# Three pace constants in the issue planner of a two-layer AdaLN transformer kernel

## The chip, the cores and the metric

The kernel runs on one core of one Trainium2 chip. The metric is the device time of one execution in microseconds (us), lower is better. Most executions of one kernel agree within 0.3%.

## The reference

The input is a batch of eight elements (called images here), each 1024 tokens of 256 features, in float32. Two transformer layers follow one another; before each part the input is normalised and modulated, and after it multiplied by a gate. Cut to what matters:

```python
# layer 0, attention: windowed ("light") plus routed ("heavy")
h = layernorm(x) * (1 + ca) + sa
light = window_attention(layernorm(h), 8 heads of 64, window 64) @ out_w
idx_q, idx_kv = top_k(coordinate_descent(h @ tok), 256)      # two routings
heavy = attention(rmsnorm(h[idx_q]), rmsnorm(h[idx_kv]), rope, 8 heads + a null key) @ out_w
x = x + ga * (light + null_token.at[idx_q].set(heavy))
# layer 0, feed-forward: 64 small functions of one variable with 16 relus each
x = x + gb * kan(layernorm(x) * (1 + cb) + sb)
# layer 1, attention: 16 heads of 16, causal, per-head layernorm on q and k, rope
x = x + ga1 * (causal_attention(layernorm(x) * (1 + ca1) + sa1) @ Wo + bo)
# layer 1, feed-forward: 256 -> 1024 -> 256, gelu, weights of two values
x = x + gb1 * (gelu(h @ bw1 + b1) @ bw2 + b2)
```

## The kernel before

After a setup of some 235 us (modulation, the routing of all images, the weights), one block of code serves all images. For each image *b* the work is cut into stages, and each stage into steps:

- `light` (windowed attention), `chain` (the end of layer 0 and the head of layer 1 for a quarter of the tokens, four quarters), `att` (causal attention, in two halves), `mlp1` (the last feed-forward, in two halves) belong to image *b*.
- `hrows` (16 steps), `heavy` (58 steps) and `hnorm` (10 steps) prepare the next image while `att` of this one runs. `hrows` gathers the routed rows; `heavy` is the routed attention; `hnorm` normalises the next image's `h`.

A planner in plain Python, `schedule()`, writes all steps of all stages into one list, `ORDER`. Each of the five engines (TensorE as PE, VectorE as DVE, ScalarE as ACT, GpSimd as POOL, and SP, which issues transfers) then issues its own part of each step in exactly this order; `take` walks the list once for each engine. So the list fixes in what order an engine meets its instructions, and semaphores alone decide when they run. An instruction that waits holds up everything behind it on its own engine.

The planner has three lanes and works in rounds. In a round lane 0 (`begin`, `start`, `light`, `att`) receives the credit `PACE`, and lanes 1 and 2 receive `SIDE`; for each full unit a lane appends one step, if its gates allow it, and loses the unit in any case:

```python
if lanes[0]:
    pace = pace_of(lanes[0][0], done.get(lanes[0][0], 0), pace)
    credit += pace
while credit >= 1.0 and lanes[0]:
    turn(0)
    credit -= 1.0
for lane in range(1, 3):
    if lanes[lane]:
        key = lanes[lane][0]
        due[lane] += SIDE[key[0], key[2]] if key[1] or key[0] != "chain" else 1.0
    while due[lane] >= 1.0 and lanes[lane]:
        turn(lane)
        due[lane] -= 1.0
```

In one image's period lane 1 holds `chain 0`, `chain 2`, `mlp1 0`, `heavy` of the next image and `mlp1 1`; lane 2 holds `chain 1`, `chain 3`, then `hrows` and `hnorm` of the next image. For the first image alone `hrows` and `heavy` stand in lane 1 beside `light 0`, and its `hnorm` is part of the setup. A period has 240 rounds. Gates that matter here: `hrows` starts when `mlp1 0` has done 6 steps; `att 1` when `mlp1 0` has done 13; `heavy` when its lane is free and `hrows` has done 12; `hnorm` when `att 1` has done 45 steps and then 11 more turns of its lane (`LAG`) have passed; `mlp1 0` when `chain 3` is done and `att 0` lacks two steps.

What the touched stages issue:

- `hrows`. POOL: steps 0 to 3 gather the four tiles of routed rows `rg` from DRAM (L2501, indirect DMA), steps 4 to 7 the rope rows (L2505), step 8 two small products (L2511, L2512), step 10 a power (L2516). DVE: steps 5 to 8 each wait for one gathered tile and sum its squares (L1820), step 9 a maximum (L1824), steps 12 to 15 scale the tiles (L1829, L1832). SP: a load of two gates at step 0 and a fill of `heavy_d` at step 12 (L2730).
- `hnorm`, twice five steps, once for each half of the tokens. DVE: two steps of statistics (L756), then the aggregate and the variance (L763, L766), then two steps of normalising (L771), which wait for POOL. POOL: at the third step of each five a power (L783), which waits for L766.
- `att 0` has 41 steps. Steps 0 to 16 are the first group's maxima, 17 to 32 the main loop; the last eight are the last product with v, the last normalisation, two transposes and four tiles of the output projection (PE L1695, DVE L2151, POOL L2653). `att 1` has 77 steps: one maximum tile ("fill": PE L1573 with L1578, reduced on DVE by L2070, L2072, L2074 or L2078) in each of the first 36, then 32 steps of the main loop (scores L1615 on PE, exp L2399 on ACT, the causal triangle L2643 on POOL, product with v L1633 on PE). The fills use two PSUM banks in turn, so a fill waits for the maximum of the fill two before it. The main loop takes four groups of eight steps, and the last four steps of a group have two triangles each; at the end of a group ACT copies the result (L2408).
- `mlp1 0` has 24 steps: 8 of normalisation, 8 of the first matrix product (PE L1710, L1711; gelu L2442 on ACT), 8 of the second (PE L1724, 16 matmuls for each of four tiles; DVE L2167; POOL L2667). At its ninth step POOL adds a bias to half the tokens (L2569, L2571).
- `heavy` begins with two memsets on DVE (L1840, L1841) that wait until `mlp1 0` is all added (L2667), and its transposes of the gathered tiles (PE L1365) wait for L1832. Later its pairs of heads are copied by DVE (L1892).

Of the kernel before, what the change touches and what calls it, by code (L numbers as in the profile page):

```python
# [64 lines left out]
def zone(base, start):  # L65
# [3 lines left out]
    def view(shape, dt=F32):  # L69
# [13 lines left out]
}  # L83


PACE = {("light", 0): (1.88, 0.9, 0.9), ("light", 1): (1.0, 1.463, 1.1), ("att", 0): (1.461, 0.9, 0.9, 0.67), ("att", 1): (1.0, 1.15, 1.15, 0.632)}

SIDE = {("chain", 0): 1.0, ("chain", 1): 1.0, ("chain", 2): 1.0, ("chain", 3): 1.0, ("heavy", 0): 1.0,
        ("mlp1", 0): 1.0, ("mlp1", 1): 0.98, ("hrows", 0): 0.8, ("hnorm", 0): 0.8}

FIRST = {('light', 0): (3.01, 0.54), ('light', 1): (1.2, 1.1)}

# [11 lines left out]
def pace_of(key, n, pace):  # L104
    if key[0] == "light":
        f = (17, 12)[key[2]]
        if key[1] == 0:
            return FIRST[key[0], key[2]][n >= f]
        return PACE[key[0], key[2]][(n >= f) + (n >= f + UNITS)]
    if key[0] == "att":  # L110
        f, g = len(first_fills(key[2])) + 1, NG * TH * (key[2] + 1)
        return PACE[key[0], key[2]][(n >= f) + (n >= f + g // 2) + (n >= f + g)]
    return pace
# [160 lines left out]
def first_fills(c):  # L274

    return [(0, *f) for f in fills(c)] + [(1, *f) for f in fills(c)[:AHEAD[c]]]
# [2624 lines left out]
```

## Time and profile before

| what | value |
|---|---|
| median of 3 runs | 4073.16 us (4068.53 to 4076.90) |
| the profiled execution's own time | 4068.53 us |
| its span, first to last instruction | 4066.8 us |
| mean granted TensorE clock | 0.91 |
| busy: PE, DVE, ACT, POOL | 83%, 60%, 48%, 36% |

The profile is of one of the three runs, the fastest. A "span" is the time from its first to its last instruction. Busy shares are averages over stages in which different engines set the pace; the questions here are answered by the order of instructions in short stretches, so most rows are from the timeline: start in us, duration in us, engine, line, operation, tiles and shapes, and in brackets the idle time of the engine before it and what ended that.

### The profile page before, as it was taken

To read this page: it belongs to the slowest core of one execution; us is meant where nothing else is said; L and a number is where in the kernel's file an instruction comes from. 1 tells how busy PE (TensorE), PEld (TensorE's weight loads), DVE (VectorE), ACT (ScalarE), POOL (GpSimd) and SP (SyncE) were. 2 spreads that over 40 slices of the span, in tenths; PEclk is the share of its full clock that TensorE was granted. 3 is DMA by queue.
4 is the path that set the end of the run, shared out by engine and by line. 5 is a ranking of instruction groups with operands and counts; after the bars stand their busy time and mean duration, and the time that the engine had idled before them with its cause. 6 is when DMAs were issued, how large, how long until landed. Compare 5 with 4: busy or idle time off the path is not lost. (4 is left out here: it accounts for less than half of the span.)

```text
span 4066.8 us, 81863 instructions
## 1 busy us (share of the span) xinstructions
PE 3382.8 (83%) x30905; PEld 2021.9 (50%) x30905; DVE 2459.2 (60%) x6188; ACT 1955.7 (48%) x4555; POOL 1476.9 (36%) x1799
## 2 busy tenths in 40 slices
PE   7368778897799878998798977998788987998787
PEld 3235554564446544465545644465444654465444
DVE  6754767466563666547573675637674575736662
ACT  5224444544364544554455542654445543645434
POOL 4123452244423542235422543235422344235411
PEclk8579889998899989998899988999899988999888
DMA  6210230002300123002400023002220024000220
GB/s 235 84 37 14 56 106 28 14 12 64 110 16 25 32 64 84 23 12 56 117 17 14 28 51 108 17 24 55 77 56 16 12 64 111 16 25 21 59 69 7
DMA packets 233603, 207.39 MB, mean 51 GB/s; under 512 B 13776, under 2 KB 214224, under 8 KB 233176
## 3 DMA queue, kind: packets, MB, share of 16 engines
q1 hardware_dynamic: 229168, 192.61, 16.9%
q0 software_dynamic: 3328, 8.39, 0.8%
q8 instruction: 252, 4.13, 0.4%
q14 instruction: 135, 1.11, 0.1%
q10 hardware_dynamic: 720, 1.15, 0.1%
HBM read 123.83 MB, written 77.69 MB: 50 GB/s over the span
## 5 line engine op out<-in xcount | busy, mean ns | idle before, releaser
L2399 ACT ACTIVATE arena<-pb 128x512 f32<-128x512 f32 (+3 forms) x1536 | 663.9, 493 | 239.2 <-PE pb L1615 232.7
L2479 POOL TENSOR_TENSOR arena<-arena,small 128x512 f32<-128x512 f32 x256 | 287.8, 1126 | 475.6 <-DVE small L1791 474.1
L2223 ACT ACTIVATE arena<-arena,small 128x256 f32<-128x256 f32 x512 | 255.8, 500 | 381.0 <-DVE small L1774 380.6
L1573 PE MATMUL pb<-arena 96*32 96x128 bf16 (+5 forms) x5280 | 371.0, 278 | 67.0 <-DVE arena L2078 24.9
L1615 PE MATMUL pb<-arena 98*32 98x512 bf16 (+3 forms) x4608 | 399.7, 340 | 31.0 <-ACT arena L2399 23.1
L1633 PE MATMUL pb<-arena,v 128*17 128x512 f32 (+3 forms) x3072 | 379.3, 498 | 22.0 <-POOL arena L2643 13.7
L2643 POOL TENSOR_SCALAR_AFFINE_SELECT arena<-arena 128x256 f32<-128x256 f32 x512 | 217.3, 428 | 474.3 <-ACT arena L2399 470.5
L2078 DVE TENSOR_REDUCE arena<-pb 128x1 f32<-128x512 f32 x512 | 334.2, 684 | 85.7 <-PE pb L1573 83.4
L1774 DVE CUSTOM_DVE_ANT_0 arena<-pb,wmask 128x256 f32<-128x256 f32 x512 | 195.7, 419 | 214.5 <-PE pb L1310 201.8
L1573 PEld LDWEIGHTS pb<-arena 96*32 96x32 bf16 (+1 forms) x5280 | 183.8, 101 | 250.7 <-issue 62.9
L1310 PE MATMUL pb<-arena 128*128 128x256 f32 x1024 | 282.9, 401 | 5.0 <-issue 2.8
L1287 PE MATMUL pb<-hTf,wqkv 128*128 128x512 f32 (+1 forms) x640 | 245.9, 536 | 23.8 <-DVE hTf L1743 12.1
L1724 PE MATMUL pb<-w2T,arena 128*128 128x256 f32 x1024 | 238.6, 384 | 12.1 <-ACT arena L2442 12.1
L1615 PEld LDWEIGHTS pb<-arena 98*32 98x32 bf16 x4608 | 139.4, 97 | 208.5 <-ACT arena L2399 113.2
L2070 DVE TENSOR_REDUCE arena<-pb 128x4 f32<-128x512 f32 x256 | 171.5, 687 | 110.7 <-PE pb L1573 101.2
L2349 ACT ACTIVATE arena<-arena,cols 128x256 f32<-128x256 f32 x256 | 148.2, 596 | 148.7 <-DVE arena L1988 147.0
L1310 PEld LDWEIGHTS pb<-arena 128*128 128x128 f32 x1024 | 188.4, 196 | 59.3 <-issue 25.8
L1724 PEld LDWEIGHTS pb<-w2T,arena 128*128 128x128 f32 x1024 | 191.3, 191 | 45.4 <-ACT arena L2442 15.8
L2539 POOL TENSOR_TENSOR arena<-arena,small 128x256 f32<-128x256 f32 x128 | 78.4, 612 | 350.8 <-DVE small L1886 349.8
L1320 PE MATMUL pb<-ident,arena 128*128 128x128 f32 x1024 | 162.9, 283 | 49.4 <-DVE arena L1784 29.4
L2072 DVE TENSOR_REDUCE arena<-pb 128x2 f32<-128x512 f32 x256 | 169.4, 685 | 28.2 <-PE pb L1573 27.9
L1578 PE MATMUL pb<-cmask,identb 128*32 128x512 bf16 (+1 forms) x640 | 118.7, 412 | 78.0 <-DMA arena<-split_k 57.1
(339 smaller groups left out, 7123.6 us busy)
## 6 DMA issues: line engine op xcount, KB each, us to landing
arena<-split_q SPq DMA_DIRECT2D x64, 384.0 KB, 3.8
arena<-split_k SPq DMA_DIRECT2D x24, 768.0 KB, 6.7
split_q<-arena SPq DMA_DIRECT2D x64, 192.0 KB, 2.1
split_q<-arena SPq DMA_DIRECT2D x96, 128.0 KB, 1.9
split_k<-arena SPq DMA_DIRECT2D x64, 192.0 KB, 2.2
split_k<-arena SPq DMA_DIRECT2D x96, 128.0 KB, 1.9
arena<-split_k SPq DMA_DIRECT2D x24, 384.0 KB, 8.5
xn<-h_d SPq DMA_DIRECT2D x8, 1024.0 KB, 9.2
```

The source lines that it names most:

```text
L1287: mm = t.matmul(bank[bk][:, 0:hi - lo], wqkv[:, k, col0:col0 + P], hT[:, k, lo:hi], start=k == 0, stop=k == KD - 1)
L1310: mm = t.matmul(bank[bk][:, j * 2 * P:(j + 1) * 2 * P], qt[:, p_, j, i * P:(i + 1) * P], kt[:, p_, i * P:i * P + 2 * P], start=True, stop= ...
L1573: mm = t.matmul(out[r:r + wide], qh[:, q0 + r:q0 + r + wide], kh_, **kw)
L1615: mm = t.matmul(bank[bk][r:r + 32, 0:w_], ka[slot(c, g)][0:KA, h, kt_ * P + r:kt_ * P + r + 32], qa[slot(c, g)][0:KA, h, q0:NH], start=Tru ...
L1633: t.matmul(bank[3][32 * h:32 * h + HD1 + 1, q0:NH], v1[:, kt_, G1 * g + h, :], pp[pn % 4][:, h % 2, 0:w_], start=kt_ == 0, stop=kt_ >= TH ...
L1724: mm = t.matmul(bank[bk][:, 0:D], g1[:, k, i * P:(i + 1) * P], w2T[:, k], start=k == 0, stop=k == FT - 1)
L1774: ins = v.tensor_tensor_reduce(out=sm[n % 2][:, j], in0=bank[n % 2][:, j * 2 * P:(j + 1) * 2 * P], in1=mk, scale=-1.0, scalar=3e38, op0=AL ...
L2078: ins = v.tensor_reduce(m[:, h, i, 3:4], bk, AX_X, ALU.max)
L2223: ins = s.activation(pm[n % 3][:, j], sm[n % 2][:, j], ACT.Exp, bias=nmx[:, 2 * sl + j:2 * sl + j + 1], scale=-1.0, accum_out=sml[:, 2 * s ...
L2399: s.activation(pp[pn % 4][:, h % 2, 0:w_], bank[n % 3][:, 0:w_], ACT.Exp).then_inc(a_exp1, 1)
L2479: g.tensor_tensor(pm[n % 3], pm[n % 3], rcl[:, 2 * sl:2 * sl + 2].unsqueeze(2).broadcast_to([P, 2, 2 * P]), ALU.mult).then_inc(p_norm0, 1)
L2643: g.affine_select(out=p2, in_=p2, pattern=[[0, 2], [1, P]], compare_op=ALU.is_ge, fill=0.0, base=0, channel_multiplier=-1).then_inc(p_tri, 1)
```

## The change

Three numbers of the planner change. Lane 0's pace in the last eight steps of `att 0` goes from 0.67 to 0.72 of a step in each round; the paces of `hrows` and of `hnorm` go from 0.8 to 1.0. No instruction is added, removed or altered; only their order in `ORDER` is.

```diff
-PACE = {("light", 0): (1.88, 0.9, 0.9), ("light", 1): (1.0, 1.463, 1.1), ("att", 0): (1.461, 0.9, 0.9, 0.67), ("att", 1): (1.0, 1.15, 1.15, 0.632)}
+PACE = {("light", 0): (1.88, 0.9, 0.9), ("light", 1): (1.0, 1.463, 1.1), ("att", 0): (1.461, 0.9, 0.9, 0.72), ("att", 1): (1.0, 1.15, 1.15, 0.632)}
 
 SIDE = {("chain", 0): 1.0, ("chain", 1): 1.0, ("chain", 2): 1.0, ("chain", 3): 1.0, ("heavy", 0): 1.0,
-        ("mlp1", 0): 1.0, ("mlp1", 1): 0.98, ("hrows", 0): 0.8, ("hnorm", 0): 0.8}
+        ("mlp1", 0): 1.0, ("mlp1", 1): 0.98, ("hrows", 0): 1.0, ("hnorm", 0): 1.0}
```

## Rows read from the trace of the kernel before

**Rows 1.** The page, part 1: busy us, share of the span, instructions.

```profile
PE 3382.8 (83%) x30905; PEld 2021.9 (50%) x30905; DVE 2459.2 (60%) x6188; ACT 1955.7 (48%) x4555; POOL 1476.9 (36%) x1799
```

**Rows 2.** The waits: waiter, releaser, us in total, times, longest us.

```profile
DVE arena L1820 <- DMA arena<-h_d,idx_all: 48.8, 18, 5.6
```

**Rows 3.** Timeline of POOL, gathers for image 2.

```profile
1065.33 0.99 POOL L2501 DMA_INDIRECT arena<-h_d,idx_all  x1 [0.27 <-POOL xt L2571]
```

**Rows 4.** Timeline of DVE in the same stretch, image 2.

```profile
1069.29 0.69 DVE L2070 TENSOR_REDUCE arena<-pb 128x4 f32<-128x512 f32 x1 [0.69 <-PE pb L1573]
...
1073.22 0.42 DVE L1820 CUSTOM_DVE_ANT_0 arena<-arena 128x256 f32<-128x256 f32 x1 [1.45 <-DMA arena<-h_d,idx_all]
...
1073.57 0.69 DVE L2070 TENSOR_REDUCE arena<-pb 128x4 f32<-128x512 f32 x1
...
1074.24 0.68 DVE L2078 TENSOR_REDUCE arena<-pb 128x1 f32<-128x512 f32 x1
```

**Rows 5.** Timeline of PE, image 2: the second product of `mlp1 0` begins.

```profile
1072.20 3.62 PE L1724 MATMUL pb<-w2T,arena 128*128 128x256 f32 x16
```

**Rows 6.** Timeline of DVE, image 3: the third and the fourth gathered tile.

```profile
1543.27 0.73 DVE L1820 CUSTOM_DVE_ANT_0 arena<-arena 128x256 f32<-128x256 f32 x1 [1.78 <-DMA arena<-h_d,idx_all]
...
1543.94 0.68 DVE L2070 TENSOR_REDUCE arena<-pb 128x4 f32<-128x512 f32 x1
1544.84 0.42 DVE L1820 CUSTOM_DVE_ANT_0 arena<-arena 128x256 f32<-128x256 f32 x1 [0.22 <-DMA arena<-h_d,idx_all]
```

**Rows 7.** Timeline of PE, image 3, the same stretch.

```profile
1544.67 0.39 PE L1573 MATMUL pb<-arena 96*128 96x512 bf16 x1 [1.54 <-DVE arena L2070]
1544.90 3.62 PE L1724 MATMUL pb<-w2T,arena 128*128 128x256 f32 x16
```

**Rows 8.** Timeline of DVE, image 2: `heavy` begins.

```profile
1089.07 0.91 DVE L1840 MEMSET arena<- 64x1024 f32 x1 [0.53 <-issue]
...
1091.24 0.35 DVE L1832 TENSOR_SCALAR arena<-arena,small 128x256 f32<-128x256 f32 x1
...
1098.91 0.74 DVE L1862 SCALAR_TENSOR_TENSOR arena<-pb,sc_all,arena 128x512 f32<-128x512 f32 x1
```

**Rows 9.** Timeline of DVE, image 3: `heavy` begins.

```profile
1561.81 0.91 DVE L1840 MEMSET arena<- 64x1024 f32 x1 [0.30 <-issue]
...
1570.64 0.74 DVE L1862 SCALAR_TENSOR_TENSOR arena<-pb,sc_all,arena 128x512 f32<-128x512 f32 x1
```

**Rows 10.** Windows, images 2 and 3: stretch, length, busy us of each engine, granted clock, DMA.

```profile
1088.00:1099.00 11.00, 7.13 (x35) 2.11 (x37) 6.07 (x11) 1.68 (x4) 0.72 (x1) 0.69 0.35 119
1560.80:1571.80 11.00, 7.27 (x44) 2.00 (x42) 6.79 (x12) 1.68 (x4) 0.68 (x1) 0.84 0.35 119
```

**Rows 11.** Timeline of DVE, image 2: `hnorm` beside `heavy`.

```profile
1197.61 0.69 DVE L1892 COPY arena<-pb 128x512 f32<-128x512 f32 x1 [0.32 <-PE pb L1425]
...
1205.45 0.36 DVE L763 BATCH_NORM_AGGREGATE small<-small 128x2 f32<-128x6 f32 x4
```

**Rows 12.** Timeline of POOL, image 2, the same stretch.

```profile
1199.17 0.41 POOL L2643 TENSOR_SCALAR_AFFINE_SELECT arena<-arena 128x256 f32<-128x256 f32 x1 [0.46 <-ACT arena L2399]
...
1206.33 1.04 POOL L783 TENSOR_TENSOR small<-small,mhalf 128x4 f32<-128x4 f32 x1
```

**Rows 13.** Timeline of PE, image 2, the same stretch.

```profile
1199.78 0.41 PE L1633 MATMUL pb<-arena,v 128*17 128x128 f32 x8
...
1202.64 1.05 PE L1633 MATMUL pb<-arena,v 128*17 128x512 f32 x8 [0.57 <-ACT arena L2408]
```

**Rows 14.** One line, PE L1260: first transposes of images 2 and 3.

```profile
L1260 PE MATMUL pb<-ident,xn x16: 272/272/273, 1228.5 to 1238.2; 128*128 128x128 f32 x16
L1260 PE MATMUL pb<-ident,xn x16: 272/272/273, 1699.9 to 1709.6; 128*128 128x128 f32 x16
```

**Rows 15.** One line, PE L1724: second product of `mlp1 0`, two images on.

```profile
L1724 PE MATMUL pb<-w2T,arena x64: 377/379/381, 1544.9 to 1559.8; 128*128 128x256 f32 x64
L1724 PE MATMUL pb<-w2T,arena x64: 377/379/381, 2010.6 to 2025.5; 128*128 128x256 f32 x64
```

## The prediction

> **What bounds the kernel now.** I began with the page: PE is busy for 83% of the span, more than any other engine [rows 1], so what delays PE tends to delay the end. Then I read the totals of the waits for the stages that the change touches; the one that matters is DVE's wait for gathered rows, 48.8 us in 18 times [rows 2]. Then the timelines of DVE, PE and POOL around `hrows`, `heavy` and `hnorm` for images 1 to 7, of which images 2 and 3 stand for the two patterns there are; then the windows for the clock; last, one line at a time for the distance between stages. The change adds and removes no work, so everything hangs on which instruction stands behind which wait.
>
> **What the new list looks like.** Count rounds from the one in which `mlp1 0` starts, as round 0. At 0.8 `hrows` starts in round 5 and skips every fifth round: in images 2, 4 and 6 its 16 steps fall in rounds 5, 6, 7, 9, 10, 11, 12, 14, 15, 16, 17, 19, 20, 21, 22, 24, in images 3, 5 and 7 in 5, 7, 8, 9, 10, 12, 13, 14, 15, 17 and so on to 24, in image 1 in 6 to 24. At 1.0 they fall in 5 to 20 without a hole. `att 1` takes one step a round from round 13, `heavy` still starts in round 24, since lane 1 is held by `mlp1 0` until then. `hnorm` opens 11 turns after round 56: at 0.8 its ten steps reach from round 69 or 70 to 81 or 82, at 1.0 from 67 to 76.
>
> **Part 1, the fourth sum of squares.** POOL's order around the gathers hardly changes: the bias of `mlp1 0` (round 8, lane 1) still precedes the fourth gather (round 8, lane 2). That gather is issued at 1065.33 [rows 3], and DVE, waiting, starts on it at 1073.22 [rows 4]: 7.9 us. In the old order of images 2, 4 and 6 the sum stands in round 15, behind three of `att 1`'s maxima. In the new one it stands in round 13, behind one. So the maximum that now runs at 1069.29 [rows 4] must wait for the tile. PE feels it: the fourth fill needs the second maximum, the fifth needs the third, and behind the fifth stands the second product of `mlp1 0`. From the sum's start to the next maximum is 0.35 us, to the one after 0.67 more [rows 4]; from that one's start to the product 0.96 (1543.94 to 1544.90) [rows 6, 7]. The product would start at 1073.22 + 1.98 = 1075.20 in place of 1072.20 [rows 5]: 3.0 us late.
>
> Images 1, 3, 5 and 7 pay part of this already. Their third gather stands behind the bias, its tile comes at 1543.27, and PE idles 1.54 us before the fifth fill [rows 6, 7]. In the new order the third tile comes sooner and the fourth takes its place: 1544.84 + 1.98 = 1546.82 against 1544.90 [rows 6, 7], 1.9 us. The fourth tile should also land somewhat sooner than now, as in image 2 (7.9 us from issue), so I take 1.5 us, with bounds 0.8 and 1.9.
>
> Is it given back? Behind the product everything up to `heavy` hangs on it: the memset starts 16.9 us after it in both images (1072.20 to 1089.07, 1544.90 to 1561.81) [rows 5, 7 to 9]. Then the patterns differ. Image 2 needs 9.84 us from the memset to the first value rows, image 3, which came 1.7 us later into its product, 8.83 [rows 8, 9], under a granted clock of 0.69 against 0.84 [rows 10]; of the two levels of 1.2 and 2.4 GHz image 2 spends more of it at the lower. I take 1.0 us back for the three images of that pattern, so 2.0 each; the bounds are 0 and 1.0. Sum of part 1: 3 x 2.0 + 4 x 1.5 = 12 us, bounds 3 x 2.0 + 4 x 0.8 = 9 and 3 x 3.0 + 4 x 1.9 = 17; if the tile is there in time it is nothing, which is a rival below.
>
> At this place the Trainium skill can be weighed. The row shows 7.9 us from issue to use [rows 3, 4]. The skill ("DMA: Bandwidth & Descriptors", Anatomy of one DMA — SWDGE (gpsimd) path) puts a transfer issued by GpSimd at about 2.0 us plus bytes over 436e3; for the 128 rows of 1 KB here that makes an estimate of 2.3 us, the tile would be there before the sum asks for it, and part 1 would cost nothing. The trace does not agree.
>
> **Part 2, the scaling of the tiles.** The last L1832 leaves the place behind `heavy`'s memsets, where it held up the next maximum by 0.35 us less its overlap [rows 8]; I take 0.26 us off in each of seven images: -1.8 us, bounds 0 and -2.4. The other steps of `hrows` move inside the second product, where PE works without a stop and DVE has room; they cost nothing while that is so. SP's fill comes three rounds earlier with nothing queued in between, POOL's power stands before instead of behind the first L2667, which it would hold up only if it came within its 1 us; its input is there at about 1074.4, the L2667 is due after 1078.
>
> **Part 3, the power of `hnorm`.** Its first power (L783) moves from round 72 or 73 to round 69. There it falls between the triangles of the last two steps of the third of `att 1`'s four groups. It waits for DVE's variance, which waits behind the copy of a pair of heads (1197.61) [rows 11]. From the aggregate's start to the power's end is 1205.45 to 1207.37, 1.9 us [rows 11, 12]. The copy ends at 1198.3, so POOL is free at 1200.2, and the last two triangles, the second of which now starts at 1199.17 [rows 12], would start at 1200.2 and about 1200.6. The product that needs them now starts at 1199.78 [rows 13] and would at about 1200.7 for its first pair and 1201.1 for its second. Behind it on PE stand the next scores, and on ACT the copy for which PE already waits 0.57 us before 1202.64 [rows 13]. I take 0.9 us for each of seven images, bounds 0.2 (ACT and PE catch up) and 1.4 (all of it stays): +6.3 us. The places are the same in all seven images. The later steps of `hnorm` move into time in which DVE idles; `start` comes in round 93, so finishing sooner gains nothing.
>
> **Part 4, 0.72 and the first image.** `att 0`'s tail takes about 11.1 rounds in place of 11.9. `mlp1 0` still waits for `chain 3`, so no stage starts sooner; a tile of the output projection slips ahead of one or two steps of `chain 3`. Zero, with 0.5 us to either side for an image. But it also shifts the fraction that lane 0 carries on, which up to now was nearly alike in all images, and so the places of `light` against `chain` in the next one. That has a price: from its first transposes to the second product of the next `mlp1 0` image 2 takes 316.4 us (1228.5 to 1544.9), image 3 310.7 (1699.9 to 2010.6) [rows 14, 15]; images 1, 2 and 7, with a lower fraction, lie at 315 to 316, the other four at 311 to 314. By hand the fractions of the new list spread over all values, about half of them in the better range, as now: 0 us, bounds -9 and +12. In the first image `heavy` starts three rounds sooner beside `light`; 0, bounds -2 and +2.
>
> **The sum.** 12 - 1.8 + 6.3 + 0 = 16.5 us, on 4068.5 for the profiled execution, 4085.0. The median of the three runs lies 4.6 us above that execution; by it, 4089.7. I say 4089.
>
> **The rivals.** (a) Gathers in time: with less in front of them the tiles land before DVE asks, or the PE queue absorbs the wait, and part 1 is worth 2 us or less. For it: the wait depends on what the 16 DMA engines have to do then, and one tile of image 1 was there without a wait. Against: six of seven images show DVE waiting for the fourth tile even in its present, later place, if only by 0.05 to 0.2 us in four of them. Sum 2 - 1.8 + 6.3 = 6.5, so 4080. (b) The power waits harmlessly (0.2 us in each image) and part 1 stands at its lower bound: 9 - 1.8 + 1.4 = 8.6, so 4082. (c) Faster: the fractions put images 1, 2 and 7 into the better range, 3 x 3.1 = -9.4 us, and the gathers land in time. This decides once parts 1 and 3 together stay under 3 us; with part 2, 4062. For it: 5.7 us between images 2 and 3 with the same instructions. Against: my count of the fractions. (d) The same mechanism to the other side: four more images in the worse range, +12.5 on the forecast, 4102. (e) The new list does what it says, but all of it in slack: 4073.
>
> **How the numbers follow.** No change is what lies within 0.2%, 8 us, about what a measurement of this kernel can tell. The forecast 0.47 (its own range 4083 to 4097), (a) and (b) 0.20, (c) 0.14, (d) 0.10, (e) 0.09. Half of (a) and (b) would read as no change, and some of the forecast's low end: slower 0.60, same 0.26, faster 0.14. The range from 4066 to 4105 leaves out about two in ten.
>
> **What would show it.** The step is right if in every image the fourth L1820 stands between the first two L2070 with a DMA wait of some 4 us before it, PE idles 2 to 3 us at the fourth and fifth fill, and L1820's total wait for the DMA grows well past 48.8 us. Part 3 is right if L783 stands before the last two L2643 of the group and L1633 waits for POOL there. The distances of rows 14 and 15, taken for all images, show part 4. Wrong would make it: a tile that lands within 5 us, or a clock that gives the stall back.

## The result and the profile after

The changed kernel is slower: 4098.26 us, median of 6 runs (4087.93 to 4111.07), against 4071.59 us (4068.43 to 4076.90, 6 runs). The ratio is 1.0078, 95% interval 1.0057 to 1.0098, which is 31.8 us on 4071, more than the 26.7 us between these medians. The record holds twelve more executions of the changed kernel, and the median of all 18 is 4102.5 us (4087.93 to 4119.38). The profiled execution took 4090.72 us, 22.2 us more than that of before; it is the second fastest of the 18, so its trace shows less of the loss than a typical execution has. I had forecast 16.5 us for it and 4089 us by the median. The six runs scatter over 23 us, all 18 over 31, those of before over 8. One execution each of `hnorm` alone (5721 us), of the late sums (9700 us) and of the kernel before beside it (9673 us) is left out of the ratios below.

Unless another view is named, rows below are from timelines: start, duration, engine, line, operation, and in brackets the idle time before. First the page after, part 1 (answers to [rows 1]), and under it a row of the totals of waits (answers to [rows 2]).

```profile
PE 3394.9 (83%) x30905; PEld 2029.7 (50%) x30905; DVE 2463.2 (60%) x6188; ACT 1955.4 (48%) x4555; POOL 1478.4 (36%) x1799
```

```profile
DVE arena L1820 <- DMA arena<-h_d,idx_all: 76.5, 27, 5.9
```

The instruction counts are the same, and PE is busy 12 us longer: part of the loss is work that ran slower, not idling. The wait for the gathered rows grew from 48.8 to 76.5 us. Where it went is seen in image 2, on POOL, DVE and PE (answers to [rows 3 to 5]):

```profile
1061.55 0.99 POOL L2501 DMA_INDIRECT arena<-h_d,idx_all  x1 [0.27 <-POOL xt L2571]
```

```profile
1065.54 0.69 DVE L2070 TENSOR_REDUCE arena<-pb 128x4 f32<-128x512 f32 x1
1069.38 0.42 DVE L1820 CUSTOM_DVE_ANT_0 arena<-arena 128x256 f32<-128x256 f32 x1 [3.15 <-DMA arena<-h_d,idx_all]
...
1069.73 0.69 DVE L2070 TENSOR_REDUCE arena<-pb 128x4 f32<-128x512 f32 x1
...
1070.40 0.69 DVE L2070 TENSOR_REDUCE arena<-pb 128x4 f32<-128x512 f32 x1
```

```profile
1070.48 0.56 PE L1578 MATMUL pb<-cmask,identb 128*128 128x512 bf16 x1 [2.55 <-DVE arena L2070]
1070.83 1.06 PE L1573 MATMUL pb<-arena 96*128 96x128 bf16 x5
1071.68 4.76 PE L1724 MATMUL pb<-w2T,arena 128*128 128x256 f32 x16
```

The fourth sum stands between the first two maxima and waits 3.15 us; the fill of PE behind it waits 2.55 us. The last of the three rows was not forecast: the 16 matmuls of the second product take 4.76 us in place of 3.62. The windows show why; columns are the stretch, its length, busy us of PE, PEld, DVE, ACT and POOL, the granted clock, DMA. First after (the stall, then the product's beginning), then before (the product's beginning):

```profile
1067.50:1070.50 3.00, 0.45 (x3) 0.03 (x2) 1.12 (x5) 0.78 (x1) 1.59 (x3) 1.00 1.08 262
1071.60:1075.10 3.50, 3.50 (x12) 2.84 (x11) 1.19 (x2) 0.00 (x0) 0.03 (x1) 0.66 0.62 219
```

```profile
1072.20:1075.70 3.50, 3.50 (x18) 2.99 (x17) 1.70 (x5) 0.78 (x1) 0.55 (x1) 1.00 1.05 270
```

PE was busy 0.45 of 3.00 us in the stall, and in the first 3.5 us of the product the granted clock is 0.66, so that much of them ran at the lower level of 1.2 GHz: 12 matmuls in place of 18.

I then measured the same distances in both traces, for all seven images, and added them up (us):

| stretch | before | after | difference |
|---|---|---|---|
| start to the first product (L1710) of image 1's stretch | 587.3 | 581.7 | -5.6 |
| first product (L1710) to second (L1724), 7 times | 95.7 | 110.1 | +14.4 |
| second product to `heavy`'s memset (L1840), 7 times | 118.3 | 123.9 | +5.6 |
| memset to the next first transposes (L1260), 7 times | 973.2 | 977.2 | +4.0 |
| first transposes to L1710, 6 times | 1801.7 | 1812.0 | +10.3 |
| last first transposes to the end | 490.5 | 484.1 | -6.5 |

The second and third lines hold the stall, the fourth `hnorm`, the last two what `light`, `chain` and `att 0` take. Of the 14.4 us of the second line 10.1 are idle time of PE (9.8 us before, 19.9 after); the rest is matmuls that ran slower.

### The profile page after: what moved, and what is told of

It is laid out like the page before. It is cut to its first block and busy times, and to the rows that moved or that the text cites. A ratio compares the mean times of both kernels' runs of the same rounds, so it can differ in the third digit from the quotient of the medians.

```text
span 4089.0 us, 81864 instructions
## 1 busy us (share of the span) xinstructions
PE 3394.9 (83%) x30905; PEld 2029.7 (50%) x30905; DVE 2463.2 (60%) x6188; ACT 1955.4 (48%) x4555; POOL 1478.4 (36%) x1799
## 3 DMA queue, kind: packets, MB, share of 16 engines
q1 hardware_dynamic: 229168, 192.61, 16.7%
## 5 line engine op out<-in xcount | busy, mean ns | idle before, releaser
L1633 PE MATMUL pb<-arena,v 128*17 128x512 f32 (+3 forms) x3072 | 382.0, 499 | 24.1 <-POOL arena L2643 15.0
L2643 POOL TENSOR_SCALAR_AFFINE_SELECT arena<-arena 128x256 f32<-128x256 f32 x512 | 216.3, 426 | 461.1 <-ACT arena L2399 457.7
L1573 PEld LDWEIGHTS pb<-arena 96*32 96x32 bf16 (+1 forms) x5280 | 185.5, 102 | 246.9 <-issue 71.3
L1287 PE MATMUL pb<-hTf,wqkv 128*128 128x512 f32 (+1 forms) x640 | 246.7, 537 | 24.4 <-DVE hTf L1743 11.5
L1724 PE MATMUL pb<-w2T,arena 128*128 128x256 f32 x1024 | 244.5, 391 | 10.8 <-ACT arena L2442 10.8
L1724 PEld LDWEIGHTS pb<-w2T,arena 128*128 128x128 f32 x1024 | 196.6, 196 | 46.2 <-ACT arena L2442 14.5
L2072 DVE TENSOR_REDUCE arena<-pb 128x2 f32<-128x512 f32 x256 | 169.6, 686 | 26.8 <-PE pb L1573 26.4
```

Source lines behind the costliest of these rows:

```text
L1287: mm = t.matmul(bank[bk][:, 0:hi - lo], wqkv[:, k, col0:col0 + P], hT[:, k, lo:hi], start=k == 0, stop=k == KD - 1)
L1573: mm = t.matmul(out[r:r + wide], qh[:, q0 + r:q0 + r + wide], kh_, **kw)
L1633: t.matmul(bank[3][32 * h:32 * h + HD1 + 1, q0:NH], v1[:, kt_, G1 * g + h, :], pp[pn % 4][:, h % 2, 0:w_], start=kt_ == 0, stop=kt_ >= TH ...
L1724: mm = t.matmul(bank[bk][:, 0:D], g1[:, k, i * P:(i + 1) * P], w2T[:, k], start=k == 0, stop=k == FT - 1)
L2643: g.affine_select(out=p2, in_=p2, pattern=[[0, 2], [1, P]], compare_op=ALU.is_ge, fill=0.0, base=0, channel_multiplier=-1).then_inc(p_tri, 1)
```

## The experiments

Theory P is the prediction's. Theory F, formed on the table above, gives the larger part to the fraction of a step that lane 0 carries into `light` (part 4). The runs below the first were timed beside 24 executions of the kernel before on the same chip; the difference is the ratio, less one, times 4071, and can differ by some us from that of the medians.

| run | median us | ratio, 95% interval | difference us |
|---|---|---|---|
| whole change | 4098.3 | 1.0078 (1.0057 to 1.0098) | +31.8 |
| `hrows` alone | 4098.5 | 1.0060 (1.0046 to 1.0074) | +24.4 |
| `hnorm` alone | 4071.2 | 0.9999 (0.9988 to 1.0009) | -0.4 |
| `att 0` tail alone | 4080.7 | 1.0026 (1.0016 to 1.0037) | +10.6 |
| `hrows` and `hnorm` | 4102.8 | 1.0068 (1.0044 to 1.0092) | +27.7 |
| `hrows`, sums two steps later | 4070.7 | 0.9994 (0.9983 to 1.0006) | -2.4 |
| `hrows`, sums one step later | 4086.9 | 1.0050 (1.0036 to 1.0065) | +20.4 |
| change, bias behind the gather | 4086.8 | 1.0041 (1.0026 to 1.0055) | +16.7 |
| before, fraction 0.42 | 4064.7 | 0.9987 (0.9976 to 0.9997) | -5.3 |
| before, fraction 0.20 | 4100.9 | 1.0068 (1.0054 to 1.0082) | +27.7 |
| change, fraction 0.42 | 4088.4 | 1.0044 (1.0027 to 1.0060) | +17.9 |
| sums two steps later, fraction 0.42 | 4061.7 | 0.9981 (0.9972 to 0.9990) | -7.7 |
| the same, bias behind the gather | 4063.6 | 0.9978 (0.9967 to 0.9989) | -9.0 |

### Each constant by itself

```diff
 # hrows alone
-("hrows", 0): 0.8
+("hrows", 0): 1.0
 # hnorm alone
-("hnorm", 0): 0.8
+("hnorm", 0): 1.0
 # att 0's tail alone
-("att", 0): (1.461, 0.9, 0.9, 0.67)
+("att", 0): (1.461, 0.9, 0.9, 0.72)
 # fourth run: hrows and hnorm
```

> Only hrows goes from 0.8 to 1.0; the fractions with which light starts are those of the kernel before. Theory P (the prediction's parts 1 and 2): the fourth sum of squares waits between the first two maxima of att 1, PE stalls at the fourth and fifth fill, +12 - 1.8 = about +10 us. Theory F (the carried fraction makes the difference): the stall is there but mostly given back before heavy, 0 to +5 us. Both: the wait of L1820 for the gathers rises from 48.8 to over 70 us.

> Only hnorm goes from 0.8 to 1.0. Theory P (part 3): the power L783 holds up two triangles in each of seven images, +6.3 us, bounds +1.4 and +9.8. Theory F: the triangles wait, but PE and ACT catch up, 0 to +3 us.

> Only the tail of att 0 goes from 0.67 to 0.72; hrows and hnorm stay at 0.8. The fractions with which light starts become those of the changed kernel (0.20 to 0.28 in images 1, 3, 4 and 6, 0.42 to 0.44 in 2, 5 and 7). Theory P (part 4): within 9 us of the kernel before, 0 as the middle. Theory F: this is the larger part of the change, +12 to +22 us, and the distance from the first transposes of an image to the next second product is 317 to 320 in images 1, 3, 4 and 6 and 310 to 314 in 2, 5 and 7.

> hrows and hnorm at 1.0, the tail of att 0 as before: the change without its third constant, with the fractions of the kernel before. Theory P: +16.5 us, like the whole change. Theory F: +3 to +9 us, and the rest of the whole change's 27 us comes from the fractions.

The three add up to +34.6 us against +31.8 for the whole, within the intervals. `hrows` costs far more than either theory gave it; its wait is 79.5 us. `hnorm` costs nothing: theory P fell there. `att 0`'s tail costs 10.6 us, under theory F's 12 and far from the forecast's 0, though inside its bounds, and `hrows` with `hnorm` cost three times what theory F gave it. With `att 0`'s tail alone, whose fractions are those of the change, the distances of rows 14 and 15 came as theory F had them but for image 3: 317.5 to 318.9 us in images 1, 4 and 6, 314.5 in image 3, 313.9 and 310.5 in images 2 and 5. So both of my theories had a part wrong, and the next runs took the two places apart.

Why `hnorm` costs nothing is seen in image 2 of its run. The power does stand before the last two triangles, and the product waits for them:

```profile
1194.81 1.04 POOL L783 TENSOR_TENSOR small<-small,mhalf 128x4 f32<-128x4 f32 x1 [0.99 <-DVE small L766]
1195.84 0.81 POOL L2643 TENSOR_SCALAR_AFFINE_SELECT arena<-arena 128x256 f32<-128x256 f32 x2
```

```profile
1196.29 0.70 PE L1633 MATMUL pb<-arena,v 128*17 128x128 f32 x6 [0.32 <-POOL arena L2643]
...
1198.98 1.05 PE L1633 MATMUL pb<-arena,v 128*17 128x512 f32 x8 [0.57 <-ACT arena L2408]
```

Counted from the memset (1085.44 here, 1089.07 before [rows 8]) the power ends at 110.4 us, where I had put it at 1200.2 - 1089.07 = 111.1; the product starts at 110.85 against 110.71 [rows 13], 0.14 us late; and the next group's product starts at 113.54 against 113.57 [rows 13], behind the same 0.57 us wait for ACT's copy. All is made up before the next wait.

### The wait of the fourth sum

```diff
 # DVE hrows, with ("hrows", 0): 1.0
-                    for _ in range(5):
+                    for _ in range(7):        # 6 for one step later
                         yield
                     for j in range(4):
...
                     v.tensor_scalar(rn, ssum, 1e-24, None, ALU.max).then_inc(v_hrn, 1)
                     yield
-                    yield
-                    yield                      # one of the two stays for one step later
 # POOL mlp1, together with the whole change
+                    yield
                     add_bias(b, c, rows[:, R_B2:R_B2 + D], gates[:, 3])
-                    for _ in range(FT):
+                    for _ in range(FT - 1):
```

> hrows at 1.0 as in the run with hrows alone, but DVE takes the sums of squares two steps later (steps 7 to 10 for 5 to 8, the maximum at step 11), so that the fourth sum stands behind three of att 1's maxima again; hnorm and att 0 as before. Theory W (the wait of the fourth sum between the maxima is the whole cost of hrows at 1.0): the 28 us are gone, the distance from the first matmul of mlp1 0's first product (L1710) to its second product (L1724) is 12.4 us in all images in place of 15.7, and the time is 4071 or some us below (the first image starts sooner, odd images lose their 1.5 us stall). Rival G (it is the earlier gathers or transfers that load something else): the time stays above 4085.

> hrows at 1.0 with DVE's sums one step later, so that the fourth sum stands behind two of att 1's maxima: between the run with hrows alone (behind one) and the one with the sums two steps later (behind three). Theory W, a wait that costs what it leaves of PE idle: L1710 to L1724 takes 13.5 to 14.3 us in all images (15.7 behind one maximum, 12.4 behind three) and the time lies between 4071 and 4098, at about 4080. Rival T (the clock falls at any stall in this place): the second product lasts longer too, L1724 to the memset over 17.5 us in most images, and the time is above 4090.

> The whole change, and on POOL the bias of mlp1 0 (L2569, L2571, 3.4 us) one step later, so that it stands behind the fourth gather instead of in front of it. The gather is issued some 3.4 us sooner. Theory W: the tile is there when DVE comes to the fourth sum or 0.5 us later, L1710 to L1724 takes about 12.4 us, and of the change's 27 us only the share of the carried fraction stays, so 4075 to 4085. Rival Q (the tile is late because of the 16 DMA engines, whenever it is asked for): the wait stays 3 us and the time about 4098.

With the sum behind three maxima the 24.4 us are gone (-2.4, from 4098 to 4071 us). Image 2 of that run on DVE, then PE:

```profile
1061.41 0.69 DVE L2068 TENSOR_REDUCE arena<-pb 128x4 f32<-128x512 f32 x1 [0.42 <-PE pb L1573]
1064.54 0.42 DVE L1820 CUSTOM_DVE_ANT_0 arena<-arena 128x256 f32<-128x256 f32 x1 [2.43 <-DMA arena<-h_d,idx_all]
```

```profile
1062.43 0.60 PE L1573 MATMUL pb<-arena 96*128 96x128 bf16 x5
1062.88 3.40 PE L1724 MATMUL pb<-w2T,arena 128*128 128x256 f32 x15
```

DVE still waits 2.43 us for the tile, but the second product started 1.66 us before the tile was there: nothing PE needs stands behind the wait. From L1710 to L1724 it is 12.4 us in six of seven images, in the run with `hrows` alone 15.7 to 16.3. (Image 7 has 14.1 without a stall: PE idles 0.5 us in all, but 15 of the 32 matmuls of L1710 and L1711 take 0.63 us, where six or seven do in the other images.) The run with `hrows` alone also has the product slowed further. Its PE, image 2:

```profile
1070.55 0.61 PE L1578 MATMUL pb<-cmask,identb 128*128 128x512 bf16 x1 [2.60 <-DVE arena L2070]
1070.95 1.06 PE L1573 MATMUL pb<-arena 96*128 96x128 bf16 x5
1071.81 6.06 PE L1724 MATMUL pb<-w2T,arena 128*128 128x256 f32 x16
```

6.06 us for 16 matmuls that take 3.62 before. Over seven images L1710 to L1724 is 111.1 us with `hrows` alone and 88.4 with the late sums, L1724 to the memset 128.5 and 118.9: 32.3 us together: 22.7 up to the product, 16.6 of them idle time of PE, and 9.6 of slower product. That is the 26.8 us between their ratios and some more; the profiled execution of `hrows` alone is the slowest of its six, 42.8 us above that of the late sums, so the two shares say what the loss is made of, not how large it is as a rule.

With the sum one step later the distance is 14.5 to 15.4 us, more than theory W said, and the time lies between the two ends, but nearer the upper one. Of theory T the trace shows little, since the product runs over 17.5 us in two images only; but this execution is the fastest of five, and by the ratio the time is 4091 us, within what T had said. So T is not excluded for the slower executions.

With the bias behind the gather the whole change takes 4086.8 us, where theory W had 4075 to 4085. The fourth gather goes out 2.3 us after L1710 in place of 5.5, and its tile is used 9.8 to 10.6 us after it in place of 13.2 to 13.8. From issue to use stays what it was, 7.5 to 8.3 us against 7.7 to 8.3. POOL, then DVE, image 2 of this run:

```profile
1060.29 0.95 POOL L2501 DMA_INDIRECT arena<-h_d,idx_all  x1 [0.30 <-issue]
```

```profile
1068.10 0.43 DVE L1820 CUSTOM_DVE_ANT_0 arena<-arena 128x256 f32<-128x256 f32 x1 [0.18 <-DMA arena<-h_d,idx_all]
```

So the tile comes sooner by what it is asked for sooner, rival Q fell, and 15.1 us of the change's 31.8 are gone. In images 1 to 3 of this execution L1710 to L1724 is 12.4 to 12.5 us, in image 4 13.4; in images 5 to 7 it is 14, and that is no stall: 14 or 15 of the first product's 32 matmuls take 0.63 us each, where in the other images seven do, and the granted clock is 0.50 over its first 8.4 us in image 5.

### The fraction that lane 0 carries into light

```diff
         if lanes[0]:
             pace = pace_of(lanes[0][0], done.get(lanes[0][0], 0), pace)
+            if lanes[0][0][0] == "light" and lanes[0][0][1] and lanes[0][0][2] == 0 and lanes[0][0] not in done:
+                credit = 0.54                  # 0.32 in the other run
             credit += pace
```

> The kernel before, with lane 0's credit set so that light starts with the fraction 0.42 in images 1 to 7. Theory F: all images in the better range, 0 to 10 us faster than before, 4062 to 4071. Rival N (the fraction does nothing, and 0.72 costs by itself): 4071.

> The same with the fraction 0.20, which images 1 and 6 of the changed kernel have. Theory F: all images in the worse range, +15 to +35 us, 4086 to 4106; distance from first transposes to the second product 317 us or more. Rival N: 4071.

> The whole change with light's start fraction at 0.42 in images 1 to 7. Theory F + W: the share of the fraction goes, the wait of the fourth sum stays, 4085 to 4095, and the distance from L1710 to L1724 stays 15.6 us. Rival (0.72 acts through the tail of att 0 and not through the fraction): 4098 as the change.

All three came out as theory F has it, though the change with 0.42 had 15.2 to 17.8 us from L1710 to L1724 in its profiled execution, not 15.6 throughout. Only the fraction differs between the first two, and 33 us (-5.3 to +27.7) lie between them. One place where it comes from, counted from the first transposes (image 2: 1222.27 with 0.42, 1234.75 with 0.20). DVE with 0.42, then with 0.20, where line numbers are two higher than in the kernel before:

```profile
1369.10 1.87 DVE L1971 TENSOR_SCALAR xn<-xt,small 128x256 f32<-128x256 f32 x2
1370.89 0.41 DVE L1776 CUSTOM_DVE_ANT_0 arena<-pb,wmask 128x256 f32<-128x256 f32 x1
```

```profile
1383.11 1.87 DVE L1971 TENSOR_SCALAR xn<-xt,small 128x256 f32<-128x256 f32 x2
1384.91 0.68 DVE L2031 TENSOR_TENSOR arena<-arena,small 128x512 f32<-128x512 f32 x1
1385.62 1.64 DVE L2033 TENSOR_TENSOR arena<-arena,tabC 128x512 f32<-128x512 f32 x1
1387.18 0.41 DVE L1776 CUSTOM_DVE_ANT_0 arena<-pb,wmask 128x256 f32<-128x256 f32 x1
```

ACT behind them, with 0.42 and with 0.20:

```profile
1371.69 0.51 ACT L2225 ACTIVATE arena<-arena,small 128x256 f32<-128x256 f32 x1 [2.81 <-DVE small L1776]
```

```profile
1387.98 0.51 ACT L2225 ACTIVATE arena<-arena,small 128x256 f32<-128x256 f32 x1 [5.09 <-DVE small L1776]
```

With 0.20 a scaling and an addition of `chain` (L2031, L2033) stand before a unit of `light`'s softmax (L1776), on which ACT's exp and then PE hang; the exp waits 5.09 us in place of 2.81. Such swaps lie all along the stage. The third addition of the `heavy` rows in `chain` (L1976), counted from the transposes, is a marker for them:

| image | 1 | 2 | 3 | 4 | 5 | 6 | 7 |
|---|---|---|---|---|---|---|---|
| fraction before | 0.32 | 0.35 | 0.38 | 0.41 | 0.43 | 0.46 | 0.26 |
| L1976 before | 185.5 | 185.3 | 181.5 | 181.3 | 182.8 | 181.0 | 185.4 |
| fraction after | 0.20 | 0.42 | 0.28 | 0.22 | 0.44 | 0.20 | 0.42 |
| L1976 after | 187.6 | 180.4 | 185.7 | 189.4 | 181.3 | 189.1 | 181.3 |
| all at 0.42 | 181.3 | 182.7 | 182.8 | 182.9 | 181.4 | 182.7 | 182.9 |
| all at 0.20 | 190.7 | 187.4 | 187.6 | 189.3 | 187.7 | 189.3 | 187.7 |

In these four executions there are three levels: 180 to 183 us from 0.38 up, 185 to 186 from 0.26 to 0.35, 187 to 191 at 0.20 to 0.22. The levels are not sharp: in the run with `hrows` and `hnorm`, with the fractions of before, images 1 and 7 have 187.0 and 188.5. The changed kernel has three images on the first, one on the second and three on the third; before had four and three. The rows of one line that answer to [rows 14, 15] say the same; image 4 after (0.22), then image 5 (0.44):

```profile
L1260 PE MATMUL pb<-ident,xn x16: 272/272/273, 2178.9 to 2188.6; 128*128 128x128 f32 x16
L1260 PE MATMUL pb<-ident,xn x16: 272/272/273, 2656.1 to 2665.8; 128*128 128x128 f32 x16
```

```profile
L1724 PE MATMUL pb<-w2T,arena x64: 377/379/381, 2500.0 to 2514.9; 128*128 128x256 f32 x64
L1724 PE MATMUL pb<-w2T,arena x64: 377/379/634, 2969.8 to 2985.7; 128*128 128x256 f32 x64
```

321.1 and 313.7 us. L1710 to L1724 takes 15.3 and 15.6 us of them, so the difference does not lie there.

### A version faster than both

> The kernel before with light's start fraction at 0.42 and hrows at 1.0 with the sums two steps later. If the two gains add, -7.6 and -1.6 us: 4062 to 4065. Rival: one takes the other's place, 4066 to 4072.

> As the run with both gains, and the bias of mlp1 0 behind the fourth gather. The tile lands 3.4 us sooner, which takes away the last short stalls before the second product: 12.4 us from L1710 to L1724 in all images, 4058 to 4064. Rival: nothing more than with both gains, or a loss because the gathers then share the queue with the loads of the next product, 4064 to 4070.

The two edits together give 4061.7 us, just under the 4062 to 4065 expected, ratio 0.9981 (0.9972 to 0.9990), and runs from 4058.8 to 4065.7 only, where the kernel before beside it had 4061.4 to 4078.3. L1710 to L1724 is 12.4 us in all seven images. Whether the gains add is not told by it: -5.3 and -2.4 make -7.7, as measured, but the second alone does not stand out from nothing. With the bias moved as well it is 4063.6 us, 0.9978 (0.9967 to 0.9989), the same within the measurement; there was no stall left to take away.

## Why the prediction was right, and where it was not

**Part 1.** The mechanism was right up to the start of the product. The fourth sum stands between the first two maxima in every image and waits 2.5 to 4.3 us (3.15 in image 2; I had said some 4), PE stalls 2.55 us in image 2, and the run with late sums shows that this is the cost. From issue to use it was 7.8 us against the 7.9 that I took over [rows 3, 4]. L1710 to L1724 grew by 14.4 us, against 3 x 3.0 + 4 x 1.5 = 15. That the sum fits so well is in part luck: image 6 was no twin of image 2 (13.7 us before, not 12.4), image 1 had no stall of image 3's kind before (PE idled 0.8 us between the two products' starts, and 16 matmuls at 0.63 us made up the rest), and in image 5 after PE idles 1.1 us where the other six have 3.0 to 3.4, behind 17 such matmuls. Wrong was the term behind it, "everything up to `heavy` hangs on it" at a fixed 16.9 us with 1.0 given back by the clock in three images: the product took 17.7 to 18.0 us in six images, +5.6, and of the 3 us to be given back between memset and value rows 0.6 came. So the clock took where I had it give; part 1 measures 19.4 us in the profiled execution (14.4 + 5.6 - 0.6) where I had 12 and an upper bound of 17. With `hrows` alone it was more again.

**The transfer.** The gather takes as long as it does because of the loads beside it. Here the DMA view of before, from 1055 to 1072 us: kind of queue, packets, MB, share of the 16 engines; then the gathers, with their median from issue to landing.

```profile
q1 hardware_dynamic: 3211, 4.09, 96.7%
q0 software_dynamic: 172, 0.51, 12.1%
...
arena<-h_d,idx_all POOLq DMA_INDIRECT x4, 7.5
```

The same view of the same kernel from 243 to 252 us, where the first image's rows are gathered:

```profile
q0 software_dynamic: 224, 0.59, 22.4%
q1 hardware_dynamic: 3, 0.00, 0.1%
...
arena<-h_d,idx_all POOLq DMA_INDIRECT x4, 3.0
```

The packets of SP's queue take 96.7% of the 16 DMA engines while the later gathers run (the two shares add to more than 100, so they are rough), and 0.1% in the first image. The Trainium skill ("DMA: Bandwidth & Descriptors", Queues, rings and completion order) says that each engine takes turns between its queues, a packet at a time, so that a gather shares each engine with what is loaded beside it. The traces agree that the load sets the time: 3.0 us from issue to landing with next to no loads beside it, and 7.5 to 8.3 us from issue to use beside SP's loads, whether the fourth gather went out 5.5 or 2.3 us after the first matmul; the turns themselves no trace here shows. The estimate of 2.3 us that the prediction took from another section of that page (Anatomy of one DMA — SWDGE (gpsimd) path) came near the first image's 3.0 us; beside the loads, where part 1 needed it, it is under a third of what the trace has.

**Part 2.** The 1.8 us were not seen. In images 3, 5, 6 and 7, which have a granted clock of 0.84 in the 11 us behind the memset in both traces, the first value rows come 9.0 to 9.1 us after it, and came 8.8 after it before. The 0.6 us gained in the sum come from images 2 and 4, where the clock was 0.69 before and is 0.84 now.

**Part 3** failed: 6.3 us forecast, -0.4 us (-4.9 to +3.7) measured, at the "power waits harmlessly" of rival (b) or below. The place was right, L783 before two L2643 and L1633 waiting for POOL. The step that failed is that the last two triangles would start at 1200.2: they started 0.7 us sooner, counted from the memset, since DVE's copy came 0.4 us sooner and only 1.7 us, not 1.9, lie between the aggregate's start and the power's end. The 0.14 us that was left went into PE's 0.57 us wait for ACT.

**Part 4** failed in size. "About half of them in the better range, as now" was a count by hand; three of seven are, and three of the other four lie at 0.20 to 0.22, in a third range that the trace of before could not show, since its fractions end at 0.26. It costs 10.6 us alone, inside the bounds of -9 and +12. In the first image `hrows` at 1.0 made the first product start 5.6 us sooner, outside my bounds of 2; without `hrows` it was 1.8 and 3.3 us sooner in the profiled executions, so up to 3.3 of the 5.6 can be a difference between executions.

So the sum was 16.5 and the profiled execution showed 22.2: a missing slower product and fractions on one side, `hnorm` and the first image on the other. That it came so near is in part luck, errors of both signs and a fast execution: by the ratio the change costs 31.8 us. The median of 4098 lies just outside the forecast's own range of 4083 to 4097 and nearer to rival (d), 4102, than to 4089. Rival (d), whose mechanism is the fractions, was half true beside the forecast; the other half is `hrows`, which cost 24.4 us where parts 1 and 2 gave it 10.

**Open.** The change's scatter goes with the clock: the fastest of its 18 executions has a mean granted clock of 0.911, the slowest 0.904. Whether other images meet the lower clock in each execution is not shown, with one trace of each kernel. Behind the memset there is a further loss. The windows of the 45 us from 15 us behind it, in images 2 and 3, before and in the fastest version:

```profile
1104.10:1149.10 45.00, 38.63 (x565) 18.44 (x558) 37.69 (x75) 24.74 (x56) 10.59 (x17) 0.92 0.01 2
1576.80:1621.80 45.00, 38.46 (x576) 18.80 (x578) 37.61 (x75) 25.19 (x58) 10.91 (x17) 0.92 0.01 2
```

```profile
1094.30:1139.30 45.00, 40.14 (x500) 17.59 (x496) 36.09 (x71) 23.18 (x49) 9.36 (x14) 0.81 0.01 2
1565.60:1610.60 45.00, 40.16 (x500) 17.19 (x496) 36.03 (x72) 23.09 (x49) 9.29 (x14) 0.81 0.01 2
```

The granted clock is 0.81 there in six of seven images of the fastest version, in five of seven of the run with late sums, in six of `hrows` alone, and in one of before and one of the whole change (a second image of before has 0.85). From the memset to the next transposes the fastest version takes 987.0 us against 973.2 before, and is faster all the same. All executions with five images or more at 0.81 have `hrows` at 1.0, but so has the whole change with one and `hrows` with `hnorm` with two. What decides it was not tried.

## What to carry to other kernels

Where a list fixes the order of issue, ask of every wait what stands behind it on its engine: a wait of 2 to 4 us for a gathered tile cost 24 us over seven images in front of two maxima that PE needed, and nothing two steps later. A pace constant acts in two ways, by its own stage and by the fraction that it leaves for the next ones; fix that fraction at a stage's start before tuning paces, or each constant is tuned against a random draw. Price a stall of PE with what the matmuls behind it then cost, not only with its length.

## What the runs showed of the hardware

- A stall of 2.6 us before the second product, with PE busy for 0.45 us of 3.00, was followed by a granted clock of 0.66 over the product's first 3.5 us, and 16 matmuls of 128x256 took 4.76 us (6.06 in another execution) in place of 3.62. The slower product added 5.6 us in one execution to 14.4 from the first product to the second, and 9.6 to 22.7 in the comparison of two others.
- The fourth indirect gather of 128 rows of 1 KB took 7.5 to 8.3 us from issue to use beside SP's loads in the changed kernel and in the run with the bias moved (up to 10.0 in the change with fraction 0.42), and moving its issue by 3.2 us moved its use by about as much. The first image's four, with no loads beside them, landed 3.0 us after issue in the median.
